# A selective scan, one state and 128 channels per unit instead of eight channels with sixteen states

## The reference, cut to what matters

```python
x = jax.nn.silu(conv)
delta = jax.nn.softplus(jnp.einsum('ble,re->blr', x, wd1) @ wd2.T + wd2_b)
Bt = jnp.einsum('ble,ne->bln', x, wb)
Ct = jnp.einsum('ble,ne->bln', x, wc)
A = -jnp.exp(A_log)
def step(h, inp):
    dt, b_t, c_t, x_t = inp
    A_bar = jnp.exp(dt[:, :, None] * A)
    h = A_bar * h + (dt * x_t)[:, :, None] * b_t[:, None, :]
    y = jnp.einsum('ben,bn->be', h, c_t)
    return (h, y)
```

## Time and profile before

| | us |
|---|---|
| median of 3 runs | 2115.75 (2113.33 to 2118.98) |
| profiled execution, its own time | 2121.68 |
| span of its records | 2119.9 |
| PE, DVE, ACT, POOL busy | 1848.2, 1660.0, 1122.1, 955.5 |
| first scan starts, last scan ends | 545.4, 780.0 |
| last `add` of the stage ends | 794.46 |

### The profile page before, as it was taken

How to read it: one execution, slowest core, us unless ns; L and a number is a source line. 1 busy time by engine, 2 the same in 40 slices (tenths; PEclk the granted TensorE clock), 3 DMA queues, 4 the chain that set the end, 5 groups by cost and what they waited for, 6 DMA issues and landing times.

```text
span 2119.9 us, 32729 instructions
## 1 busy us (share of the span) xinstructions
PE 1848.2 (87%) x12452; PEld 1202.0 (57%) x12452; DVE 1660.0 (78%) x2131; ACT 1122.1 (53%) x1868; POOL 955.5 (45%) x365
## 2 busy tenths in 40 slices
PE   6899999985888887799999978889888777999998
PEld 5444454464444446576777645555555454677776
DVE  4566556468899989577767699989999999777666
ACT  2354545534533323345555567777777766555554
POOL 3365555522566641100000088888989889400000
PEclk8799999998999998799999999989999999999999
DMA  3111211000200001101000000000000000100000
GB/s 85 31 31 41 52 32 32 2 12 9 41 1 0 0 1 35 34 1 47 30 16 16 1 1 1 1 2 2 2 1 31 2 2 2 42 19 31 16 15 21
DMA packets 35682, 39.14 MB, mean 18 GB/s; under 512 B 5892, under 2 KB 22535, under 8 KB 35527
## 3 DMA queue, kind: packets, MB, share of 16 engines
q1 hardware_dynamic: 34998, 36.01, 6.8%
q10 hardware_dynamic: 528, 1.05, 0.2%
HBM read 21.05 MB, written 1.05 MB: 10 GB/s over the span
## 4 chain that ended last, share of the span: by engine, by line
PE 49%; issue 19%; DVE 19%; POOL 7%; ACT 4%; DMA 1%; SPq 1%; DVEq 0%; ACTq 0%; POOLq 0%; PEldq 0%
PE ps L46 10%; PE ps L47 8%; PE ps L48 8%; DVE negm L2663 6%; PE ps L532 3%; PE ps L548 2%; PE ps L581 2%; PE ps L573 2%; POOL AF L1574 2%; DVE AF L2670 2%; PE ps L2492 2%; PE ps L2575 1%; POOL hc L1574 1%; POOL AR_plain L2468 1%; PE ps L938 1%
## 5 line engine op out<-in xcount | busy, mean ns | idle before, releaser
L2663 DVE TENSOR_REDUCE negm<-ps 128x64 bf16<-128x1024 f32 x256 | 302.1, 1214 | 20.2 <-PE ps L2566 20.0
L2468 POOL TENSOR_TENSOR AR_plain<-AF 128x2048 f32<-128x2048 f32 x64 | 261.9, 4096 | 31.4 <-ACT AF L2619 31.3
L46 PE MATMUL ps<-XH,AR 128*128 128x512 f32 x616 | 256.4, 416 | 14.6 <-DVE XL L251 4.0
L2627 ACT ACTIVATE AF<-ps 128x1024 f32<-128x1024 f32 x192 | 196.4, 1023 | 133.7 <-PE ps L2575 132.3
L755 POOL TENSOR_TENSOR AF<-AF 128x2048 f32<-128x2048 f32 (+3 forms) x52 | 184.8, 3553 | 179.0 <-ACT AF L695 175.7
L47 PE MATMUL ps<-XL,AR 128*128 128x512 f32 x616 | 246.5, 400 | 0.0
L48 PE MATMUL ps<-XH,AR 128*128 128x512 f32 x616 | 246.5, 400 | 0.0
L2575 PE MATMUL ps<-negm,ident_bf 128*128 128x512 bf16 x512 | 161.4, 398 | 80.4 <-DVE negm L2663 80.0
L695 ACT ACTIVATE AF<-ps 128x512 f32<-128x512 f32 (+1 forms) x304 | 153.9, 576 | 144.4 <-PE ps L532 68.9
L2670 DVE TENSOR_REDUCE AF<-AF 128x128 f32<-128x2048 f32 x96 | 218.4, 2275 | 0.0
L285 POOL TENSOR_SCALAR var_eps<-mv 128x8 f32<-128x8 f32 x10 | 4.2, 422 | 371.7 <-DVE mv L262 371.6
(11 more groups left out here) (338 smaller groups left out, 4355.4 us busy)
## 6 DMA issues: line engine op xcount, KB each, us to landing
AR<-AR SPq DMA_DIRECT2D x96, 128.0 KB, 2.4
AF<-in_L_ffn_Wg_dram SPq DMA_DIRECT2D x21, 256.0 KB, 2.7
AF<-in_L_ffn_Wu_dram SPq DMA_DIRECT2D x21, 256.0 KB, 3.1
AF<-in_L_ffn_Wd_dram SPq DMA_DIRECT2D x21, 256.0 KB, 3.8
AF<-AF SPq DMA_DIRECT2D x16, 64.0 KB, 2.4
AF<-AR_plain SPq DMA_DIRECT2D x16, 64.0 KB, 2.4
AF<-in_L_attn_a_Wq_dram SPq DMA_DIRECT2D x1, 512.0 KB, 4.0
AF<-in_L_attn_a_Wout_dram SPq DMA_DIRECT2D x1, 512.0 KB, 9.0
```

Of the source, the lines that this page charges most:

```text
L46: pe.matmul(out, ah, bh, start=start, stop=False)
L2468: pool.tensor_tensor(p6[m % 3].rearrange("p (j q i) -> p j q i", j=HJ, i=2), e6[m % 4].rearrange("p (j q i) -> p j q i", j=HJ, i=2), w6i[: ...
L2627: act.activation(o[:, :, q0:q0 + 2 * SUB], bank(2 * (j % 3), 2).rearrange("p (j c) -> p j c", j=HJ), ACT.Exp).then_inc(s6_e, 1)
L2663: dve.tensor_reduce(negm6[:, j % 4, :], bank(2 * (j % 3), 2).rearrange("p (j q i) -> p q j i", j=HJ, i=2), mybir.AxisListType.XY, ALU.max, ...
```

## The change

**A unit is now one state of 128 channels.** There are NJ = 2 x 16 pairs j (batch b, state n), each with EC = 2 units (channel halves c), again 64 units.

- The decays need no spreading: ACT takes exp of delta from SBUF to SBUF, with A of this state as its scale (`decay`).
- The inputs delta x B need B of this state at each time, the same for all channels. So PE transposes delta x once per batch (`turn_x`, taken over by ACT's `take_turned` into `dxT`) and B (`turn_b`, into `bT`): time now lies on the partitions, in 8 blocks of 128. Per pair j the 8 blocks of 128 x 256 are multiplied by a per-partition B: 6 blocks by ACT (`inputs_first`), one by DVE (`inputs_middle`), one by POOL (`inputs_last`). PE transposes them back, 8 transposes of 128 x 128 per unit into PSUM (`drive`), where the scan reads them.
- DVE has the scan alone per unit, and one 128 x 256 product per pair.
- The outputs need C of this state at each time on all 128 partitions. SP issues one DMA per pair j that copies row 80 + n of `dtr[b]` to 128 partitions, 512 KB, into one of four buffers `crow`. POOL multiplies both scans of the pair by it.
- `collect` adds the products of 16 states in PSUM: per unit two fp32 matmuls of 512 columns with the identity.
- `high`, `high_x`, the low parts, `spread` and `gather` fall away. Three buffers hold decays and scans where two did.

```diff
-        NU = NP * NG
+        NJ = B * NS
+        NU = EC * NJ
...
-        bbs = [tf(L), tf(L)]
-        ccs = [tf(L), tf(L)]
+        crow = [tf(L), tf(L), tf(L), tf(L)]
...
+        dxT = [tp(LB, E2), tp(LB, E2)]
+        inputs = [tp(LB, E2), tp(LB, E2)]
+        dx = tp(EC, L)
...
+        hcs = [hc[:, 0, :], hc[:, 1, :], uu[:, 0, :], uu[:, 1, :]]
+        hss = [hs[:, 0, :], hs[:, 1, :], pre[:, 0:L]]
+        decays = [xp_a[:, 0, 0:L], xp_a[:, 1, 0:L], dA[:, 0, :]]
...
+        READY_AT = {9: (2, 0), 11: (2, 1), 15: (3, 0), 17: (3, 1)}
+        SOFT_AT = {2 + n: (2 + n // 3, n % 3) for n in range(6)}
+        TURN_AT = {EC * 11 + c: c for c in range(EC)}
...
         def s2_load(q, s):
-            for b in range(B):
+            for j in range(NJ):
+                b, n = j // NS, j % NS
                 q.wait_ge(s2_drc, 2 * b + 2)
-                wait(q, s2_bd, 16 * EG * b)
-                wait(q, s2_cd, 16 * EG * b)
-                for e in range(EG):
-                    q.dma_start(bbs[b][NS * e:NS * e + NS], dtr[b][DT:DT + NS]).then_inc(s2_bd, 16)
-                for e in range(EG):
-                    q.dma_start(ccs[b][NS * e:NS * e + NS], dtr[b][DT + NS:XB]).then_inc(s2_cd, 16)
+                wait(q, s2_hc, EC * (j - 3))
+                q.dma_start(crow[j % 4].unsqueeze(1),
+                            dtr[b][DT + NS + n:DT + NS + n + 1, :].unsqueeze(1).to_broadcast([1, P, L])).then_inc(s2_cd[j % 4], 16)
...
+            def inputs_last(j):
+                b, n = j // NS, j % NS
+                pool.wait_ge(s2_xtc, EC * (b + 1))
+                pool.wait_ge(s2_btc, b + 1)
+                wait(pool, s2_u, EC * (j - 1))
+                pool.tensor_tensor(inputs[j % 2][:, LB - 1, :], dxT[b][:, LB - 1, :],
+                                   bT[b][:, LB - 1, n:n + 1].to_broadcast([P, E2]), ALU.mult).then_inc(s2_up, 1)
+
+            inputs_last(0)
+            inputs_last(1)
+            for k in range(NU):
+                j = k // EC
+                pool.wait_ge(s2_h, k + 1)
+                pool.wait_ge(s2_cd[j % 4], 16 * (j // 4 + 1))
+                wait(pool, s2_yg, k - 3)
+                pool.tensor_tensor(hcs[k % 4], hss[k % 3], crow[j % 4], ALU.mult).then_inc(s2_hc, 1)
+                if k % EC == 0 and j + 2 < NJ:
+                    inputs_last(j + 2)
+                if k in READY_AT:
+                    ready(*READY_AT[k])
...
+            def turn_x(b, c):
+                pe.wait_ge(s2_mul, EC * b + c + 1)
+                for t in range(LB):
+                    ins = pe.transpose(bank(2 * c, 2)[:, P * t:P * t + P], dx[:, c, P * t:P * t + P], ident[:, :])
+                ins.then_inc(s2_xt, 1)
+
+            def drive(k):
+                j, c = k // EC, k % EC
+                if c == 0:
+                    pe.wait_ge(s2_ua, E_ACT * (j + 1))
+                    pe.wait_ge(s2_ud, j + 1)
+                    pe.wait_ge(s2_up, j + 1)
+                if k in TURN_AT:
+                    pe.wait_ge(s2_xtc, EC + TURN_AT[k] + 1)
+                wait(pe, s2_h, k - 1)
+                for t in range(LB):
+                    ins = pe.transpose(bank(2 * c, 2)[:, P * t:P * t + P], inputs[j % 2][:, t, P * c:P * c + P],
+                                       ident[:, :])
+                ins.then_inc(s2_u, 1)
+
+            def collect(k):
+                b, n, c = k // (EC * NS), k // EC % NS, k % EC
+                pe.wait_ge(s2_hc, k + 1)
                 if n == 0:
                     pe.wait_ge(s2_zc, 4)
+                    if b:
+                        pe.wait_ge(s2_y2, c + 1)
+                    elif c:
+                        pe.wait_ge(s2_btc, 2)
                 for i in range(2):
+                    ins = pe.matmul(bank(4 + 2 * c + i), ident[:, :], hcs[k % 4][:, 512 * i:512 * i + 512],
+                                    start=n == 0, stop=n == NS - 1)
+                ins.then_inc(s2_yg, 1)
...
+            def inputs_first(j):
+                b, n = j // NS, j % NS
+                act.wait_ge(s2_xtc, EC * (b + 1))
+                act.wait_ge(s2_btc, b + 1)
+                wait(act, s2_u, EC * (j - 1))
+                for t in range(E_ACT):
+                    act.activation(inputs[j % 2][:, t, :], dxT[b][:, t, :], ACT.Identity,
+                                   scale=bT[b][:, t, n:n + 1], bias=0.0).then_inc(s2_ua, 1)
+
+            def decay(k):
+                b, n, c = k // (EC * NS), k // EC % NS, k % EC
+                act.wait_ge(s2_add, EC * b + c + 1)
+                wait(act, s2_h, k - 2)
+                act.activation(decays[k % 3], dl[b][:, c, :], ACT.Exp,
+                               scale=negA[:, NS * c + n:NS * c + n + 1]).then_inc(s2_dA, 1)
...
+            for j in range(NJ):
+                if j + 1 < NJ:
+                    decay(EC * (j + 1))
+                if j + 2 < NJ:
+                    inputs_first(j + 2)
+                if j + 1 < NJ:
+                    decay(EC * (j + 1) + 1)
+                if j in SOFT_AT:
+                    soft(*SOFT_AT[j])
+                for c in range(EC):
+                    if EC * (j + 1) + c in TURN_AT:
+                        take_turned(1, c)
...
+            def inputs_middle(j):
+                b, n = j // NS, j % NS
+                dve.wait_ge(s2_xtc, EC * (b + 1))
+                dve.wait_ge(s2_btc, b + 1)
+                wait(dve, s2_u, EC * (j - 1))
+                for t in range(E_ACT, LB - 1):
+                    ins = dve.tensor_scalar(inputs[j % 2][:, t, :], dxT[b][:, t, :], bT[b][:, t, n:n + 1], None,
+                                            ALU.mult)
+                ins.then_inc(s2_ud, 1)
...
-                wait(dve, s2_h, k - 1)
-                dve.wait_ge(s2_px, k + 1)
-                if k % (EC * NG) == 0:
-                    dve.wait_ge(s2_bd, 16 * EG * (k // (EC * NG) + 1))
-                dve.tensor_tensor(uu[:, k % 2, :], bank(4, 2), bbs[k // (EC * NG)], ALU.mult).then_inc(s2_u, 1)
                 dve.wait_ge(s2_u, k + 1)
                 dve.wait_ge(s2_dA, k + 1)
-                wait(dve, s2_hc, k - 1)
-                dve.tensor_tensor_scan(hs[:, k % 2, :], bank(2 * (k % 2), 2), uu[:, k % 2, :], 0.0,
+                wait(dve, s2_hc, k - 2)
+                dve.tensor_tensor_scan(hss[k % 3], decays[k % 3], bank(2 * (k % EC), 2), 0.0,
                                        ALU.mult, ALU.add).then_inc(s2_h, 1)
-                if k % NG == 1 and k > NG:
-                    gate(k // NG - 1)
+                if k == 1:
+                    dve.wait_ge(s2_bt, 2)
+                    dve.tensor_copy(bT[1].rearrange("p t n -> p (t n)"), bank(6)[:, 0:LB * NS]).then_inc(s2_btc, 1)
+                if k % EC == EC - 1 and k // EC + 2 < NJ:
+                    inputs_middle(k // EC + 2)
```

More of the change, by code:

```diff
@@ L1463, in build @@
         s2_drc = sem("s2_drc")
-        s2_bd = sem("s2_bd")
-        s2_cd = sem("s2_cd")
+        s2_cd = [sem("s2_cd%d" % i) for i in range(4)]
         s2_z = sem("s2_z")
@@ L1569, in s2_pool @@
-            for u in range(NU):
-                pool.wait_ge(s2_h, u + 1)
-                if u % (EC * NG) == 0:
-                    pool.wait_ge(s2_cd, 16 * EG * (u // (EC * NG) + 1))
-                wait(pool, s2_yg, u - 3)
-                pool.tensor_tensor(hcs[u % 4], hs[:, u % 2, :], ccs[u // (EC * NG)], ALU.mult).then_inc(s2_hc, 1)
-                if u // NG + 1 < NP:
-                    ready(u // NG + 1, u % NG)
+                    pool.wait_ge(s2_mul, p)
+                    pool.wait_ge(s2_xt, EC)
@@ L1646, in s2_pe, with turn_b @@
-            delta(0)
-            x_project(1)
-            delta(1)
-            def decay(k):
-                p, n = k // NG, k % NG
-                c, g = p % EC, ORDER[n]
+            def turn_b(b):
+                if b:
+                    pe.wait_ge(s2_zc, 4)
+                else:
+                    pe.wait_ge(s2_ina, 16)
+                for t in range(LB):
+                    ins = pe.transpose(bank(6)[:, NS * t:NS * t + NS], dtr[b][DT:DT + NS, P * t:P * t + P],
+                                       ident[DT:DT + NS, DT:DT + NS])
+                ins.then_inc(s2_bt, 1)
@@ L1676, in collect @@
-            def collect(k):
-                pe.wait_ge(s2_hc, k + 2)
-                if k % NG == 0:
-                    wait(pe, s2_y2, k // NG)
-                for i in range(2):
-                    for m in range(2):
-                        g = ORDER[k % NG + m]
-                        j, r = g // 4, g % 4
-                        ins = pe.matmul(bank(6 + i)[32 * j:32 * j + 32, :], gather[:, r, :],
-                                        hcs[(k + m) % 4][:, 512 * i:512 * i + 512], start=r == 0, stop=r == 3)
-                ins.then_inc(s2_yg, 2)
+                    ins = pe.matmul(bank(4 + 2 * c + i), ident[:, :], hcs[k % 4][:, 512 * i:512 * i + 512],
+                                    start=n == 0, stop=n == NS - 1)
@@ L1696, in project @@
                 ins.then_inc(s2_o, 1)
```

(28 more changed lines are left out.)

185 lines of the change are left out of this document (64 added, 121 removed).

## The result

The changed kernel takes 2391.47 us (median of 4 runs, 2383.14 to 2395.1), the kernel before 2117.36 (4 runs): a ratio of 1.129, 95% interval 1.1255 to 1.1328. It is slower, as forecast, but by 274 us and not by 389: 2391 lies under the range of 2430 to 2640. The profiled execution took 2383.14 us, with a span of 2381.3 at a mean granted clock of 0.902.

The account below looks back on a forecast made before the run. DVE bounded the old kernel; single-partition C-row reads would bound the new one. 32 rows at 19.8 us plus tail end the stage at 1177.7 instead of 794.46, +383 on 2121.68: 2505 us, range 2430 to 2640.

Parts of the forecast that it names:

- 32 rows at 19.8 us without a gap end at 524.5 + 2 + 635: Scan: C rows, first issued at 524.45, land after 2 us latency and 635 us of back-to-back transfers, ending at 1161.5.
- the partition's neighbours matter: Sign in the scan: they matter if the C rows change pace from one group of states to the next.
- The tail: After the last C row: two POOL products, 4.0 us, then collect, gate, projection and adds, 12.2 us; stage ends at 1177.7.
- at most 2 us more: Tail after the scan: PE, idle most of each row, may work at half its clock, costing at most 2 us.
- The longer preparation: Ahead of the scan: more softplus, products and transposes; first scan within 3 us of 545.4, covered by the DMA, costed at nothing.
- ACT's six products: Scan, per pair: six ACT products of 256 columns, taken at 0.34 us each; with two exps ACT's pair is 4.2 us.
- PE's pair: Scan: PE's work per pair, about 2.8 us per unit, 5.6 us, where a pair takes 7.3 now.
- `lnt` behind the rows: SP queue: two loads stage 3 needs land some 4 us behind row 31, inside 16 us of tail; costed at nothing.
- Rival 1: C rows: DMA not limited by the partition read, rows in 1.8 to 3 us, PE decides; 2074 us, chance 0.09.
- Rival 2: Scan: rows are quick but POOL blocks DVE's product, 7.2 us per pair; no change, 2122 us, chance 0.02.
- Rival 3: C rows: one partition slower than its group, 30 us per row, 2830 us; with anything over 24 us, chance 0.05.
- milder limit, 6 to 17.5 us per row: C rows: case of rows at 6 to 17.5 us, still slower, 2130 to 2430 us, chance 0.04.

Follow-up runs that it names:

- e1: The changed kernel with each 512 KB C-row transfer read from 128 partitions of one tile instead of one partition (output not the reference's): 2084.5 us.
- e5: The changed kernel with C rows 0 to 3 loaded over and over, all from partitions 80 to 83 (output not the reference's): 2495.3 us.
- e3: The changed kernel with states reordered (0, 4, 8, 12, 1, ...), so the four C rows in flight lie in four different groups of four partitions: 2176.6 us.
- e6: The changed kernel with states in the order 0, 4, 1, 5, ..., so consecutive C rows alternate between two groups of four partitions: 2205.2 us, one run.
- e11: The kernel of e3 with a wait on SP that allows at most two C rows in flight instead of four: 2223.4 us, one run.
- e10: The changed kernel with one more wait on SP: a C row is issued only when the row before has landed: 2542.5 us, one run.
- e4: The changed kernel with each batch's 16 C rows written to DRAM once and every row broadcast from there to 128 partitions: 2082.4 us.
- e12: The kernel of e4 with ACT making five of the eight input blocks instead of six and DVE two instead of one: 2121.2 us.
- e9: The changed kernel with C rows copied to 8 places in SBUF and each row filled by eight 64 KB transfers, each from one partition: 2116.8 us.

## Why the prediction was right and wrong

**The mechanism and the direction were right**: the term that decides is the C rows, the read side is the limit (e1), nothing else of the pair matters, and the DMA share near 1 at some 25 GB/s is there wherever a single group is read (27 GB/s). The rate itself was well chosen too: 19.8 us per row from what four of 16 partitions gave, and 19.4 measured where only one group is read (e5). The Trainium skill's port rule, which gave 19.3, agrees with e5 within 1%.

**The step that failed** is "32 rows at 19.8 us without a gap end at 524.5 + 2 + 635": it multiplies one row's time by 32, as if a single reader served all rows. But rows under way at the same time in different groups of four partitions are read at once, mostly two of them (e3, e6, e11), and without a second row under way the gain is gone (e10). The states in order cross from group to group at rows 4, 8, 12, and again at the turn to `dtr[1]` (row 15 in partition 95, row 16 in partition 80), seven times in all, and there 27 GB/s becomes about 50. Against 4 x 19.4 us per group, the first two crossings gave 3 and 9 us, and each of the other five 17 to 20. The prediction wrote both halves down, the 104 GB/s of 16 partitions that it divided among four groups read at once and, in its last sentence, "the partition's neighbours matter", and didn't put them in the sum. In numbers, each from a row above:

- From the first issue to POOL's first product of the last row: 1039.57 - 519.55 = 520.0 us, forecast 637.0: -117.0. Of it 32 x 0.4 = 13 us is the rate of one row (19.4 for 19.8), the other 104 the overlap. e5, which has the rate and no overlap, is 2495.3 - 2391.5 = 104 us above the change: the same number by another way (100 if each is taken against its own runs of the kernel before).
- The tail, from that product to the stage's end at 1062.27: 22.7 us, forecast 16.2: +6.5. The last unit's scan was late (POOL waited 2.35 us for it), since PE was still collecting row 30 at half its clock, four matmul records in 3.78 us where e4 has them in 1.88: +2.3 us until POOL is through. Then the last collects stood behind batch 0's projection on PE (+2.4), and the last gate behind batch 0's adds and the other gate on DVE (+1.4), where the forecast had one gate alone. The half clock cost about the "at most 2 us more"; the order of the work behind it wasn't in the sum.
- The profiled execution came to the stage 4.9 us earlier than the one of before, took 6.4 us less behind it, and lies 8.3 us under the median: -3.0 together.
- Sum: -117.0 + 6.5 - 3.0 = -113.5 us, the whole distance from 2505 to 2391.5.

**The rest, by its steps.** The longer preparation: the first scan starts at 540.51, 20.96 us behind SP's first C issue, as long as the 20.95 us of before (545.4 less the 524.45 of the earlier trace rows); right. DVE's product 0.35 us, forecast 0.3; right. ACT's six products: 2.50 us, forecast 2.04; too low, without effect here. POOL's idle time ahead of its product: 349 us in all, forecast 490, wrong by the same step; and it is put down to "issue", where a DMA was to be named. PE's pair: 5.2 to 5.9 us in e4, forecast 5.6. `lnt` behind the rows: both loads are issued by 1026, the DMA engines stand still from 1040 on and nothing in stage 3 waited; right.

**The rivals.** Rival 1, no limit by the source partition, 2074: wrong for this change, but its sum for what PE's pace would give comes within 11 us of what e1 and e4 measured, 2084 and 2082. Rival 2 (POOL blocks DVE's product): the blocking is real, but it sets no pace with one product per pair, which mostly fits in front of POOL's next; two don't (e12). That e12 came out at its 2122 is luck: the rival let one product wait for three of POOL's, in e12 the second of two waits for one. The trace agrees with the Trainium skill's exclusive lock that the loser waits out ("SBUF — State Buffer", section "SBUF: two separate sides"): 2.08 us for a product of 0.33. Rival 3, a partition slower than its group: wrong, 19.4 us and not 30. The "milder limit, 6 to 17.5 us per row" had 0.04, and that is where the measurement lies, though by a mechanism (two readers part of the time) that the case didn't name. The bounds of one row's rate, 17.5 to 24, were taken as bounds of the average of 32; they had to be wider on the fast side, since nothing in the profile said that rows don't overlap.

## What to carry to other kernels

A broadcast by DMA from one SBUF partition is paid where it is read, 27 GB/s for all copies together, and more rows in flight don't help as long as they read the same four partitions: multiply by the number of copies before you write it. Here it was better to write the rows to DRAM once (1.9 us for a batch's 64 KB) and to broadcast from there: 512 KB landed in 3.6 us, instead of 20.9 alone and 54 to 64 with four under way. And when a rate is a property of a place, ask of a sequence of transfers which of them lie in different places before multiplying one's time by their number.

## What the runs showed of the hardware that was not expected

- Transfers of one queue overlap, mostly in pairs, when they read different groups of four partitions: 9.9 us per row with two groups, 8.9 with four, 19.4 with one. Two in flight from two groups each landed in 20.9 us, as one does alone (e11, e10). Eight sources in turn gave 76 GB/s (e9).
- Rows of 4 KB in DRAM, each read 128 times, moved at 369 GB/s over 3 us (e4), more than the 290 of the weight load in the earlier trace rows.
- The profile puts POOL's wait for late DMAs down to "issue" for 309 of its 349 us; the landings and the windows' GB/s showed it, not the releaser.
- Two short DVE products in a row cost 1.8 us per pair more than one where the scan runs freely, 1.2 on average, by where the second falls against POOL's instruction (e12).
